# Four-layer graph network on one core: projection steps moved by half rows, a small product moved to GpSimd, kept columns and the last chunk's finish reordered

## The reference

```
x1 = LN(x  + adj @ (scale * (adj @ (x @ w0))) + bias0)
x2 = LN(x1 + relu((inv_deg * (A' @ x1)) @ W1.T + b1))        A' = alpha*adj + (1-alpha)*I
z  = leaky_relu((D adj D x2) @ wz + bz)                       D = 1/sqrt(row sums)
S  = exp(-dist(z_i, z_j)/2), only the 4 largest in each row kept
A2 = S + adj
x3 = LN(x2 + (D2 A2 D2 x2) @ w2 + b2)                         D2 = 1/sqrt(row sums of A2)
out = LN(x3 + relu([x3, adj @ x3] @ W3.T + b3))
```

## Time and profile before

| | |
|---|---|
| three runs | 1420.53, 1424.22, 1425.78 us; median 1424.22 |
| profiled execution, own time | 1423.97 us |
| its span in the trace | 1422.4 us |
| TensorE busy | 1385.7 us (97%) |
| VectorE busy | 849.1 us (60%) |
| ScalarE busy | 452.7 us (32%) |
| GpSimd busy | 236.0 us (17%) |
| TensorE granted clock, mean | 0.999 |

### The profile page before, as it was taken

The page is one execution under the profiler, slowest core; times in us unless marked ns, Lnnn a source line. Parts: engine busy times, 40 slices in busy tenths (PEclk is TensorE's granted clock), DMA queues, the critical chain, the costliest instruction groups (busy, mean ns, idle before and its releaser), DMA issues.

```text
span 1422.4 us, 20428 instructions
## 1 busy us (share of the span) xinstructions
PE 1385.7 (97%) x7365; PEld 794.7 (56%) x7365; DVE 849.1 (60%) x1324; ACT 452.7 (32%) x958; POOL 236.0 (17%) x356
## 2 busy tenths in 40 slices
PE   7999999999999999999999999999999999999998
PEld 6888887877544444544445445444444444444467
DVE  7877766666323433434323359999999846655144
ACT  5767665655300000000010136655555410000011
POOL 2111110110100100000000000111111167776000
PEclk9999999999999999999999999999999999999999
DMA  9999998887999879987787812203444699999863
GB/s 348 393 376 386 357 329 327 319 301 268 335 388 355 348 303 391 412 356 297 291 325 277 307 31 89 89 16 119 133 134 133 237 391 403 404 379 403 353 244 115
DMA packets 111699, 407.53 MB, mean 287 GB/s; under 512 B 11696, under 2 KB 28080, under 8 KB 90112
## 3 DMA queue, kind: packets, MB, share of 16 engines
q1 hardware_dynamic: 79520, 316.43, 59.9%
q0 software_dynamic: 19728, 73.71, 13.3%
q10 hardware_dynamic: 12368, 16.26, 3.2%
HBM read 339.77 MB, written 66.58 MB: 286 GB/s over the span
## 4 chain that ended last, share of the span: by engine, by line
PE 66%; DVE 19%; DMA 7%; POOL 4%; issue 2%; ACT 1%; SPq 0%; DVEq 0%; POOLq 0%; ACTq 0%
PE acc L1262 10%; PE acc L1264 10%; PE acc L1263 10%; DVE hT L1145 8%; PE pt L1330 5%; DVE wT L1146 4%; DMA region<-in_adj 4%; POOL gath_all L605 4%; DVE wz_sb L1146 3%; PE pt L1264 3%; PE pt L1262 3%; PE pt L1263 3%; PE acc L1310 3%; PE acc L1312 2%; PE acc L1314 2%
## 5 line engine op out<-in xcount | busy, mean ns | idle before, releaser
L1330 PE MATMUL pt<-ident,region 128*128 128x128 f32 x1024 | 244.0, 279 | 13.5 <-DMA region<-in_adj 12.6
L1330 PEld LDWEIGHTS pt<-ident,region 128*128 128x128 f32 x1024 | 200.4, 196 | 40.8 <-issue 7.7
L1262 PE MATMUL acc<-region,yop 128*128 128x512 f16 (+1 forms) x581 | 217.8, 375 | 4.0 <-DVE yop L880 2.7
L1264 PE MATMUL acc<-region,yop 128*128 128x512 f16 (+1 forms) x581 | 217.5, 374 | 0.0
L1263 PE MATMUL acc<-region,yop 128*128 128x512 f16 (+1 forms) x581 | 217.5, 374 | 0.0
L1082 DVE SCALAR_TENSOR_TENSOR region<-pt,region 128x512 f16<-128x512 f32 x200 | 136.2, 687 | 75.5 <-ACT region L671 74.9
L718 ACT ACTIVATE region<-pt 128x512 f32<-128x512 f32 x256 | 133.0, 603 | 114.5 <-PE pt L1426 46.4
L671 ACT ACTIVATE region<-pt 128x512 f16<-128x512 f32 x200 | 118.1, 596 | 110.1 <-PE pt L1330 99.6
L1145 DVE MAX8 hT<-region 128x8 f32<-128x4096 f32 x31 | 136.8, 4412 | 2.3 <-ACT region L718 2.3
L1419 PE MATMUL pt<-yop 128*128 128x512 f16 x256 | 97.9, 382 | 8.6 <-ACT region L718 7.5
L639 ACT ACTIVATE std<-mv,eps_ln 128x4 f32<-128x4 f32 x31 | 9.2, 297 | 280.0 <-DVE mv L889 280.0
(11 more groups left out here) (257 smaller groups left out, 2278.8 us busy)
## 6 DMA issues: line engine op xcount, KB each, us to landing
region<-at_scratch SPq DMA_DIRECT2D x163, 1280.0 KB, 8.0
region<-in_adj SPq DMA_DIRECT2D x128, 512.0 KB, 7.6
at_scratch<-region POOLq DMA_DIRECT2D x40, 768.0 KB, 6.7
at_scratch<-region POOLq DMA_DIRECT2D x40, 512.0 KB, 6.8
region<-at_scratch SPq DMA_DIRECT2D x76, 256.0 KB, 2.7
x_scratch<-xout ACTq DMA_DIRECT2D x16, 256.0 KB, 10.8
region<-at_scratch ACTq DMA_DIRECT2D x3, 1280.0 KB, 9.8
gath_all<-x_scratch POOLq DMA_DIRECT2D x12, 256.0 KB, 5.3
```

The costliest lines, as they stand in the source:

```text
L1262: nc.tensor.matmul(into, y[:, 0, kt, :], high, start=(kt == first_tile), stop=False)
L1264: return nc.tensor.matmul(into, y[:, 1, kt, :], high, start=False, stop=(kt == last_tile))
L1330: ins = nc.tensor.transpose(pt[kt % 4][:, t * P:(t + 1) * P], nat[u % 4][:, t, b * BLOCK + j:(b + 1) * BLOCK:PAIR], ident[:, :])
```

## The change

Seven edits:

1. Projection steps 0 to 8 stood at the half rows (ahead), 1, 2, 4, 5, 7, 8, 10, 11; they now stand at 2, 3, 4, 6, 7, 8, 10, 11, 12.
2. The product `dinv2y` goes from VectorE's `inverse(g)` to the start of GpSimd's `scales(g)`.
3. After the last group's Exp, ScalarE runs a Sqrt over one column, with a result that nobody reads.
4. On ScalarE the last chunk's second `hT` copy stands behind the first half's square root and store.
5. Last chunk: the bias enters PSUM as a matmul of the identity with the bias, and VectorE's add of the bias goes; relu and residual read PSUM directly.
6. In the same place, the products with the turned x3 no longer wait for `hT`.
7. `KEPT5`: kept column 2 goes from ahead of u=2 to ahead of u=1, column 3 from u=3 to u=2, column 4 from u=4 to u=3.

```diff
-PROJECTION_AT = {1: 1, 2: 2, 4: 3, 5: 4, 7: 5, 8: 6, 10: 7, 11: 8}
+PROJECTION_AT = {2: 0, 3: 1, 4: 2, 6: 3, 7: 4, 8: 5, 10: 6, 11: 7, 12: 8}
...
             def scales(g_tiles, g):
+                step(nc.gpsimd.tensor_scalar(dinv2y[:, g_tiles], dinv2[:, g_tiles], 1.0 / Y_SCALE[3], None, ALU.mult))
                 nc.gpsimd.tensor_tensor(S[:, g_tiles, :], S[:, g_tiles, :], dinv2y[:, g_tiles].unsqueeze(2)
                                         .to_broadcast([P, TPC, TOP]), ALU.mult).then_inc(S_scaled, 1)
...
                 nc.scalar.activation(S[:, tiles_g, :], S[:, tiles_g, :], ACT.Exp, scale=-0.5).then_inc(S_ready, 1)
+                if g == NCH - 1:
+                    nc.scalar.activation(std[:, 0:1], eps_ln[:, 0:1], ACT.Sqrt)
...
-            projection_step(0)
             for i in range(1, KT + TPC + 1):
...
             act_finish(act, 5, NCH - 2)
-            sums_half(1)
             for h in range(2):
                 half = slice(h * TPC // 2, (h + 1) * TPC // 2)
+                if h == 1:
+                    sums_half(1)
                 act.wait_ge(var_ready, nth(XIN, 5, NCH - 1) + h)
...
                 dve.wait_ge(nat_full, n)
-                nc.vector.tensor_tensor(t_nat[:, half, :], late_nat[:, half, :], bias[5][:, :].unsqueeze(1).to_broadcast([P, TPC // 2, D]),
-                                        ALU.add).then_inc(nat_read, 1)
+                dve.wait_ge(x3_loaded[(NCH - 1) % X3_BUFFERS], 16 * ((NCH - 1) // X3_BUFFERS + 1))
+                nc.vector.scalar_tensor_tensor(t_nat[:, half, :], late_nat[:, half, :], 0.0,
+                                               gath[(NCH - 1) % X3_BUFFERS][:, half, :], ALU.max, ALU.add
+                                               ).then_inc(nat_read, 1)
                 dve.wait_ge(nat_read, n)
...
-                step(nc.vector.reciprocal(dinv2[:, g_tiles], droot[:, g_tiles]))
-                nc.vector.tensor_scalar(dinv2y[:, g_tiles], dinv2[:, g_tiles], 1.0 / Y_SCALE[3], None, ALU.mult
-                                        ).then_inc(dinv_ready, 1)
+                nc.vector.reciprocal(dinv2[:, g_tiles], droot[:, g_tiles]).then_inc(dinv_ready, 1)
...
-            KEPT5 = [[0], [1], [2], [3], [4, 5], [6]]
+            KEPT5 = [[0], [1, 2], [3], [4], [5], [6]]
...
             def project_half(h):
                 n = nth(ALL, 5, NCH - 1) + h
-                pe.wait_ge(hT_ready, n)
                 pe.wait_ge(xT_ready, nth(XTS, 5, NCH - 1))
                 pe.wait_ge(nat_read, n - 1)
-                for t in range(TPC)[h * TPC // 2:(h + 1) * TPC // 2]:
-                    nc.tensor.matmul(late_nat[:, t, :], xT[:, t * P:(t + 1) * P], wT[:, 1, :], start=True, stop=False)
-                    last = nc.tensor.matmul(late_nat[:, t, :], hT[:, t * P:(t + 1) * P], wT[:, 2, :], start=False, stop=True)
+                half = range(TPC)[h * TPC // 2:(h + 1) * TPC // 2]
+                nc.tensor.matmul(late_nat[:, half[0]:half[-1] + 1, :], ident[:, :],
+                                 bias[5][:, :].unsqueeze(1).to_broadcast([P, TPC // 2, D]), start=True, stop=False)
+                for t in half:
+                    nc.tensor.matmul(late_nat[:, t, :], xT[:, t * P:(t + 1) * P], wT[:, 1, :], start=False, stop=False)
+                pe.wait_ge(hT_ready, n)
+                for t in half:
+                    last = nc.tensor.matmul(late_nat[:, t, :], hT[:, t * P:(t + 1) * P], wT[:, 2, :], start=False, stop=t == half[-1])
                 last.then_inc(nat_full, 1)
```

More of the change, by code:

```diff
@@ L1014, in last_half @@
                 dve.wait_ge(nat_full, n)
-                nc.vector.tensor_tensor(t_nat[:, half, :], late_nat[:, half, :], bias[5][:, :].unsqueeze(1).to_broadcast([P, TPC // 2, D]),
-                                        ALU.add).then_inc(nat_read, 1)
+                dve.wait_ge(x3_loaded[(NCH - 1) % X3_BUFFERS], 16 * ((NCH - 1) // X3_BUFFERS + 1))
+                nc.vector.scalar_tensor_tensor(t_nat[:, half, :], late_nat[:, half, :], 0.0,
+                                               gath[(NCH - 1) % X3_BUFFERS][:, half, :], ALU.max, ALU.add
+                                               ).then_inc(nat_read, 1)
                 dve.wait_ge(nat_read, n)
-                dve.wait_ge(x3_loaded[(NCH - 1) % X3_BUFFERS], 16 * ((NCH - 1) // X3_BUFFERS + 1))
-                step(nc.vector.scalar_tensor_tensor(t_nat[:, half, :], t_nat[:, half, :], 0.0,
-                                                    gath[(NCH - 1) % X3_BUFFERS][:, half, :], ALU.max, ALU.add))
                 for t in range(TPC)[half]:
```

## The result

The changed kernel took 1416.80 us (median of 10 executions, 1414.21 to 1419.73), the kernel before 1424.52 us (10 executions, 1420.53 to 1427.48). The ratio is 0.9939, 95% interval 0.9925 to 0.9953: faster by 0.61%; the interval just takes in half a per cent (0.995), so that the gain is more than that is likely, not certain. The profiled execution took 1415.13 us, with a span of 1413.6.

The account below looks back on a forecast made before the run. TensorE is nearly always busy, so time can come only from its few waits or an engine holding it back, VectorE in the search. Terms 2.05 + 1.3 + 2.85 + 0.3 = 6.5 us gave 1417.7 us, range 1414.8 to 1420.8.

Parts of the forecast that it names:

- Projection steps: Search, first rows: ScalarE's root of group 0 ends 2.05 us earlier; bounds 1.3 and 3.45 us.
- The small product: Search, rows with an inverse: 0.19 us off VectorE, seven times, 1.3 us won; bounds 0 and 1.75.
- The line of half a per cent: Whole kernel: 7.1 us is about what measurement can tell, line at 1417.1; chances faster 0.40, same 0.58, slower 0.02.
- The root's table: Last group's root: the table load already runs ahead of the wait, so the edit wins 0.
- What follows the search: TensorE's work after row 31's release and the chain to the gathers move 3.35 us earlier.
- rival two: Pass 5, u=1: the gathers don't follow the earlier search, only 4.2 us won, 1420.0 us; chance 0.14.
- Rival three: Pass 4: DMA engines set the pace, the search's 3.35 us are lost, 1421.0 us; chance 0.08.
- Kept columns: Pass 5: column 2 ahead of u=1 removes TensorE's wait for chunk 4, 2.85 us won; bounds 0 and 2.85.
- The end: Last chunk: 0.44 us lost, 0.3 and 0.46 won, so 0.3 us less; bounds +0.4 and -1.0.
- Rivals one: Search: VectorE's two waits go fully, more is won, 8.5 us, 1415.7 us; chance 0.20.
- four: Search: through the shared port pair GpSimd's product delays scans by 0.3 us each, losing 2 us, 1421.1; chance 0.03.
- five: Store of y falls behind a ring load, gathers start 8.9 us later, kernel slower at 1425.5 us; chance 0.03.

Follow-up runs that it names:

- e5: Changed kernel without the extra Sqrt, with ScalarE's root of a group ahead of the projection step at the same row's end; 1418.57 us (one execution).
- e1: Kernel before with only the projection steps' new places; 1425.44 us, ratio 0.9993.
- e6: e5 with projection steps 0 and 1 half a row earlier each; 1416.87 us (one execution).
- e9: Changed kernel with the old order of the kept columns; 1423.05 us, ratio 0.998.
- e12: Changed kernel with the small product back on VectorE; 1420.12 us, ratio 0.996.
- e2: Kernel before with only the small product moved to GpSimd; 1422.42 us (one execution).
- e4: Kernel before with only the last chunk's edits (bias by TensorE, products ahead of the wait, ScalarE's order); 1423.64 us (one execution).
- e3: Kernel before with only the new order of the kept columns; 1422.49 us, ratio 0.9976.
- e8: e6 with the first half of the last chunk as in the kernel before; 1415.91 us, ratio 0.9926.
- e10: e8 with kept column 3 also ahead of u=1; 1415.41 us, ratio 0.9941.
- e7: Kernel before with kept column 1 moved behind u=1, for a longer wait there; 1431.05 us, ratio 1.0041.
- e11: Changed kernel unaltered, timed once more; 1417.14 us, ratio 0.9943.

## Why the prediction was right, and where it was not

The predicted 1417.7 us is 0.9 above the measured median, inside the range, and the sum of 6.5 us stands beside 6.62 in the traces. The total is in part luck: 1.05 us too much for the projection steps was made up by 0.26 more from the small product and by 0.85 of shorter waits in pass 4, which the prediction did not have and which no run ties to the change. The result lies over the line of half a per cent, to which I gave 0.40; why it is more than the 6.62 us is argued at the end of this part.

**Projection steps: 2.05 us predicted, 1.00 measured.** The step that failed is "Before there are two of the first kind and one of the second up to row 5, after the change three of the first: 0.43 us less." It took a half row with a step as one without a wait. Step 0 is only a turning, 0.44 us, and covers the 1.17 us at the end of a row but in part: after the change there are four waits (0.68, 0.58, 0.74, 0.74), 2.74 us against 2.65 before. These 0.5 us are one half of the error. The whole of it can be read from ScalarE's timeline, where a half row runs from one start of four copies to the next. Before, the empty half row at the end of row 3; in the changed kernel, the one with step 0:

```profile
870.33 2.07 ACT L718 ACTIVATE region<-pt 128x512 f32<-128x512 f32 x4 [1.34 <-PE pt L1426]
874.66 2.06 ACT L718 ACTIVATE region<-pt 128x512 f32<-128x512 f32 x4 [2.27 <-PE pt L1426]
...
849.92 2.07 ACT L719 ACTIVATE region<-pt 128x512 f32<-128x512 f32 x4 [1.72 <-PE pt L1426]
854.26 2.07 ACT L719 ACTIVATE region<-pt 128x512 f32<-128x512 f32 x4 [1.77 <-PE pt L1426]
```

The first takes 4.33 us, the second 4.34: exchanging the empty place for a turning gains nothing, where the prediction's terms give 0.73 (1.17 less 0.44). A middle of a row that loses its full step takes 3.79 us instead of 4.44 (row 1) or 4.39, a gain of 0.65 where the terms give 0.79 (1.53 less 0.74). And row 1's first copies start 0.36 us earlier (+12.59 for +12.95), not 0.53 (0.58 less 0.05). In sum 0.65 + 0.36 = 1.01 us. e5 shows what then decided: ScalarE's two copies of step 6 ahead of the root, 0.97 us, which my working had treated as given. The decider was named rightly (the root, with "still a short wait"); the bounds were not: 1.00 lies under the lower one of 1.3.

**The small product: 1.3 us predicted, 1.56 measured.** The first of the seven groups gave 0.21 us, between the reciprocal and the scan of row 5, the other six 1.35. That is 0.22 for each group instead of 0.19: 0.19 in the row of the inverse, and 0.02 to 0.03 in the row behind it (8.85 us instead of 8.87), which I had not counted. No scan grew.

**The root's table: 0 predicted.** From the last search to the last reciprocal VectorE stood idle for 4.39 to 4.40 us in the kernels without the extra Sqrt (before, e1 to e6), and for 4.48 to 4.50 in those with it (both profiles of the changed kernel, e9, e12): the extra Sqrt costs 0.09, the load was hidden before. The edit wins nothing.

**What follows the search.** 2.56 instead of 3.35. GpSimd's first gather moved by 3.04, chunk 4 by 2.86, so rival two did not come true. TensorE gained 0.85 us more by shorter waits in pass 4; this made up for the missing part. Rival three is out with it, though loads there still land in 16.0 us.

**Kept columns: 2.85 predicted, 2.85 measured** in this pair. The margin behind chunk 4 is 0.54 us instead of 1.05, because TensorE moved more than chunk 4 did.

**The end: 0.3 predicted, 0.34 measured**, by the two amounts forecast (0.44 lost in the first half, 0.78 won in the second).

**Rivals one, four and five.** One names a time near the result (1415.7), but not for its reason: both waits of VectorE are still there. Scans beside GpSimd took 4.39 to 4.42 us, and the Trainium skill's rule of an exclusive lock (SBUF — State Buffer, section "SBUF: two separate sides") does not bear on these scans here. The gathers came earlier, not 8.9 us later.

**The line of half a per cent.** The prediction set the profiled execution against the median, 0.25 us apart, and took it as typical. By its time it was, by its clock not: its mean granted clock rounds to 0.999 and it holds no slow stretch at all. Of 71 executions of the kernel before that ran beside the experiments, 54 had a mean of 0.998 or less, with a mean time of 1426.39 us; the other 17 took 1424.06. One stretch of 3.4 us at 0.50 lowers the mean of the span by 3.4 x 0.5 / 1424 = 0.0012. Three digits tell this only roughly: the profiles of e2 and e4, with one stretch each, have 0.998, those of e3 and e9, also with one, 0.999. Of the 16 executions of the changed kernel 14 had 0.999 or 1.000, with 1417.02 on average: 7.0 us under those 17. The remaining 1.5 us of the difference in means (8.5) come with executions at a lower mean clock; that the clock is their cause fits, but no run changes the clock alone. Over all kernels, with a wait of about 3 us at u=1 left in (before, e1, e9) 69 of 93 executions had 0.998 or less; with it taken out (the changed kernel, e3, e8, e10, e12) 10 of 51.

That accounting closes in single profiles too. Take u=1's start, add before's 160.39 us (156.49 if the column is already done) and e2's 1.68 where the clock falls, and take off 0.34 for the new end:

| profile | wait at u=1 | clock behind it | u=1 starts | by this sum | measured |
|---|---|---|---|---|---|
| changed | none | 1.00 | +421.65 | 577.80 | 577.80 |
| e1 | 3.0 | falls | +426.00 | 588.07 | 588.07 |
| e3 | none | 1.00 | +427.02 | 583.51 | 583.51 |
| e4 | 3.1 | falls | +424.30 | 586.03 | 586.03 |
| e5 | 1.0 | 1.00 | +421.69 | 577.84 | 577.86 |
| e9 | 4.0 | falls | +422.40 | 584.13 | 584.13 |

**What stays open.** First, waits for the ring in pass 4: 1.6 to 3.5 us in the six profiles with the product on VectorE (mean 2.4), 0.8 to 2.3 in the eight with it on GpSimd (mean 1.5). A link would make the product worth more than its 1.6 us, but the two ranges overlap, e12's time does not exclude 1.6, and no run changes these waits alone. Second, the clock at row 31: it fell in three of the six profiles whose wait there is 1.71 us (e1, e3, e7) and in none of the eight with 1.50, and e12's times speak against a firm link. Third, what spreads the zero point from 833.18 to 840.34; of e11's 6.8 us some 1.7 are a fall of the clock in the first stage (0.61 in the window from 172 to 176, 0.96 in the one before), the rest has no such place.

## What to carry to other kernels

Price a wait of the engine that is otherwise always busy with the clock behind it, not by its length alone, and look at the mean granted clock of every timed execution before taking the profiled one as typical (0.999 can still hide one slow stretch in 1420 us). When an early stage is made faster, compute again what the waits behind it become: here the one at u=1 was 2.7 us in the profile of the kernel before and 4.0 behind the faster search (one profile each). In a hand-written order, a half row filled with a short piece can take as long as an empty one (4.34 and 4.33 us here), and a small instruction that others wait for should stand ahead of copies that nobody needs yet.

## What the runs showed of the hardware that I had not expected

- **A short wait can halve TensorE's clock for a while.** Behind waits of 3.00, 3.1, 3.32 and 4.02 us (e1, e4, e2, e9) the granted clock was 0.50 for about 3.4 us, and each fall cost 1.68 us; with 2.69 us (before) and 1.05 us (e5) it stayed at 1.00. At row 31 of the search, where TensorE had short pauses in every row and then one of 1.71 us, it fell in three of six profiles. With 6.67 us of wait (e7) it was low before the wait was over.
- **The first 835 us are not repeatable.** In fourteen profiles with the same code there, they took 833.18 to 840.34 us; behind them the same kernel repeats within 0.01 us in the two profiles taken. A difference of two spans (8.8 us here) is therefore worth less than the difference counted from the last common point (6.62).
- **A product of 128x4 cost about the same on either engine.** It took 0.21 us of VectorE's time with its wait for the reciprocal, and 0.22 to 0.25 us on GpSimd (e2, changed kernel).
